# Storing tile 13 of a 16-tile head in two halves

## The chip, the cores and the metric

The kernel runs on one core of a Trainium2 chip. The metric is the device time of one execution in microseconds (us), the median of several runs.

## The reference

```
users, items = interactions[:, 0], interactions[:, 1]          # 2048 pairs
all_embed = concatenate([users_emb_w[users], items_emb_w[items]], axis=1)   # 32 + 32
h = relu(all_embed @ w1.T + b1)                                 # 128
h = relu(h @ w2.T + b2)                                         # 128
cross = one_hot(items, 1250)
return sigmoid(concatenate([cross, h], axis=1) @ w_head.T + b_head)   # 2048 x 1250 f32
```

The product with the one-hot part is a choice of one row of the head's weights. So each pair needs a gathered row of 1250 numbers, the product of h with the remaining 128 columns of the head, the bias, and a sigmoid. 10.24 MB of output are written.

## The kernel before, in words

The 2048 pairs are 16 tiles of 128 (t = 0 to 15, LAST = 15). For each tile GpSimd issues two indirect DMAs (L167, L171): one brings the item's embedding and its 1250 head numbers, the other the user's embedding, into the tile's part of `rows`. Every tile has its own 1250 columns there, `logits(t)`; the sum, the sigmoid and the store all work in that place. A gather is issued when the one four tiles before it has landed.

VectorE splits the embedding into two parts of fewer bits (L206, L208), TensorE transposes it (L301), VectorE copies it back (L212). TensorE then does layer 1 (L309, L310), ScalarE relu 1 (L262), TensorE layer 2 (L314), ScalarE relu 2 twice, once rounded (L266) and once in full (L271), and VectorE takes their difference (L216). The head is four passes over 1250 columns, in chunks of 512, 512 and 226, into one of two PSUM accumulators (L318). VectorE adds the gathered row (`add_rows`, L221), ScalarE applies the sigmoid (`sigmoid`, L275), and SyncE, which waits for the sigmoid, issues the store (L144).

The order on each engine is written out by hand. For t = 1 to 14, ScalarE does relu 1 and relu 2 of tile t+1 and then the sigmoid of tile t-1, so that the sigmoid of tile 13 stands behind both layers' relus of tile 15. VectorE does the sum of tile t-1, the preparation of tile t+2 and then the difference for tile t+1.

The end is written differently. Tile 14 is added, put through the sigmoid and stored in two halves of 625 columns (L240, L288, L148). Tile 15 goes in three chunks, for which TensorE computes one chunk after the other (`last_head`, L350), VectorE adds (L244), ScalarE applies the sigmoid (L292), and the chunks are stored by SyncE (L152) and, the last, by ScalarE's own queue (L295). SyncE issues stores strictly in order, each behind its wait; its last wait is for all stores to have landed (L153).

Of the kernel before, what the change touches and what calls it, by code (L numbers as in the profile page):

```python
# [7 lines left out]
SLOTS = 2  # L8
IN_FLIGHT = 4
WARM = 6  # L10

ALU = mybir.AluOpType
ACT = mybir.ActivationFunctionType
# [5 lines left out]
def rec_head_kernel(nc, pairs, user_rows, item_rows, w1T, b1, w2T, b2, w_hiddenT, b_head, out):  # L19
# [5 lines left out]
    H2, N = w_hiddenT.shape  # L25
# [3 lines left out]
    TILES = B // P  # L29
    LAST = TILES - 1  # L30
# [2 lines left out]
    chunks = [(c, min(BANK, N - c)) for c in range(0, N, BANK)]  # L33
    halves = [(0, N // 2), (N // 2, N - N // 2)]
    BANKS = len(chunks)
    assert B % P == 0 and H1 == P and H2 == P and 2 * K1 == P and item_rows.shape[1] == ITEM_ROW
    assert BP * BC == N and TILES > IN_FLIGHT

# [4 lines left out]
    with ExitStack() as ctx:  # L43
# [6 lines left out]
        def sem(name):  # L50
            return ctx.enter_context(nc.semaphore(name))
# [60 lines left out]
        s_acc = sem("s_acc")  # L112
        s_sum = sem("s_sum")
        s_prob = sem("s_prob")
        s_out = sem("s_out")
        s_half_sum = sem("s_half_sum")
        s_half_prob = sem("s_half_prob")
        s_last_acc = sem("s_last_acc")
        s_last_sum = sem("s_last_sum")
        s_last_prob = sem("s_last_prob")  # L120

        def embedding(t):
            return rows[:, t * ROW:t * ROW + K1]
# [1 line left out]
        def logits(t, c=0, n=N):  # L125
            return rows[:, t * ROW + K1 + c:t * ROW + K1 + c + n]
# [3 lines left out]
        @block.sync  # L130
        def _(sp):
            sp.dma_start(idx[:], pairs_v).then_inc(s_idx, 16)
            sp.dma_start(bias_f[:], bias_v).then_inc(s_bhead, 16)
            for half in range(2):
                sp.dma_start(w1T_f[half * K1:(half + 1) * K1, :], w1T).then_inc(s_w1, 16)
            sp.dma_start(w2T_sb[:], w2T).then_inc(s_w2, 16)
            sp.wait_ge(s_const, 3)
            sp.wait_ge(s_bias_split, 2)
            for r, part in enumerate((bias_hi, bias_lo)):
                sp.dma_start(bias_parts[r:r + 1, :].bitcast(F32).rearrange("a (p c) -> a p c", p=BP),  # L140
                             part[:].bitcast(F32)).then_inc(s_bias_row, 16)
            for t in range(LAST - 1):
                sp.wait_ge(s_prob, t + 1)
                sp.dma_start(out_v[:, t * N:(t + 1) * N], logits(t)).then_inc(s_out, 16)  # L144

            for i, (c, n) in enumerate(halves):
                sp.wait_ge(s_half_prob, i + 1)
                sp.dma_start(out_v[:, (LAST - 1) * N + c:(LAST - 1) * N + c + n],  # L148
                             logits(LAST - 1, c, n)).then_inc(s_out, 16)
            for i, (c, n) in enumerate(chunks[:-1]):  # L150
                sp.wait_ge(s_last_prob, i + 1)
                sp.dma_start(out_v[:, LAST * N + c:LAST * N + c + n], logits(LAST, c, n)).then_inc(s_out, 16)  # L152
            sp.wait_ge(s_out, 16 * (LAST - 1 + len(halves) + BANKS))  # L153

        @block.gpsimd
        def _(pool):
# [19 lines left out]
        @block.vector  # L176
        def _(dve):
            nc.vector.memset(warm_pe[:], 0.0).then_inc(s_warm_pe, 1)  # L178
            nc.vector.memset(warm[:], 0.0).then_inc(s_const, 1)
            nc.vector.memset(bias_sel[:].bitcast(F32), 0.0).then_inc(s_const, 1)  # L180
            nc.vector.memset(bias_parts[:].bitcast(F32), 0.0).then_inc(s_const, 1)
            dve.wait_ge(s_const, 3)
            nc.vector.memset(bias_sel[0:2, :].bitcast(F32), 1.0).then_inc(s_const, 1)
            dve.wait_ge(s_bhead, 16)
            nc.vector.tensor_copy(bias_hi[:], bias_f[:]).then_inc(s_bias_split, 1)
            dve.wait_ge(s_bias_split, 1)
            nc.vector.tensor_tensor(bias_lo[:], bias_f[:], bias_hi[:].bitcast(F32),
                                    ALU.subtract).then_inc(s_bias_split, 1)
            dve.wait_ge(s_w1, 32)
            nc.vector.tensor_copy(w1T_hi[:], w1T_f[:]).then_inc(s_w1_parts, 1)  # L190
            dve.wait_ge(s_w1_parts, 1)
            nc.vector.tensor_tensor(w1T_lo[:], w1T_f[:], w1T_hi[:].bitcast(F32), ALU.subtract).then_inc(s_w1_parts, 1)

            def split_hidden():

                dve.wait_ge(s_hid_hi, 1)
                dve.wait_ge(s_hid_f, 1)
                nc.vector.tensor_tensor(w_hid_lo[:], acc[1][:, 0:N], w_hid_hi[:].bitcast(F32),
                                        ALU.subtract).then_inc(s_hid_lo, 1)

            def split_emb(t):
                dve.wait_ge(s_rows[t], 32)
                if t >= 1:

                    dve.wait_ge(s_xT, t)
                nc.vector.tensor_copy(emb[:, 0:K1].bitcast(F32R), embedding(t)).then_inc(s_emb_hi, 1)  # L206
                dve.wait_ge(s_emb_hi, t + 1)
                nc.vector.tensor_tensor(emb[:, K1:2 * K1], embedding(t), emb[:, 0:K1], ALU.subtract).then_inc(s_emb, 1)  # L208

            def copy_embT(t):  # L210
                dve.wait_ge(s_xT, t + 1)
                nc.vector.tensor_copy(embT[:], ps_x[:, 0:P]).then_inc(s_embT, 1)  # L212

            def split_h2(t):
                dve.wait_ge(s_h2, t + 1)
                nc.vector.tensor_tensor(h2T_lo[t % SLOTS][:], h2T_f[:], h2T_hi[t % SLOTS][:].bitcast(F32),  # L216
                                        ALU.subtract).then_inc(s_h2_lo, 1)

            def add_rows(t):
                dve.wait_ge(s_acc, t + 1)  # L220
                nc.vector.tensor_tensor(logits(t), acc[t % SLOTS][:, 0:N], logits(t), ALU.add).then_inc(s_sum, 1)  # L221

            split_emb(0)
            copy_embT(0)
            split_hidden()
            split_emb(1)
            copy_embT(1)
            split_h2(0)
            split_emb(2)
            copy_embT(2)  # L230
            split_h2(1)
            for t in range(1, LAST):
                add_rows(t - 1)
                if t + 2 < TILES:
                    split_emb(t + 2)
                    copy_embT(t + 2)
                split_h2(t + 1)
            dve.wait_ge(s_acc, LAST)
            for c, n in halves:
                nc.vector.tensor_tensor(logits(LAST - 1, c, n), acc[(LAST - 1) % SLOTS][:, c:c + n],  # L240
                                        logits(LAST - 1, c, n), ALU.add).then_inc(s_half_sum, 1)
            for i, (c, n) in enumerate(chunks):
                dve.wait_ge(s_last_acc, i + 1)
                nc.vector.tensor_tensor(logits(LAST, c, n), acc[LAST % SLOTS][:, c:c + n], logits(LAST, c, n),  # L244
                                        ALU.add).then_inc(s_last_sum, 1)

        @block.scalar
        def _(act):
# [11 lines left out]
            def relu_1(t):  # L260
                act.wait_ge(s_l1, t + 1)
                nc.scalar.activation(h1T[:], ps_h[:, 0:P], ACT.Relu, bias=b1_sb[:]).then_inc(s_h1, 1)  # L262
# [7 lines left out]
                    act.wait_ge(s_h2_lo, t)  # L270
                nc.scalar.activation(h2T_f[:], ps_h[:, P:2 * P], ACT.Relu, bias=b2_sb[:]).then_inc(s_h2, 1)  # L271

            def sigmoid(t):
                act.wait_ge(s_sum, t + 1)
                nc.scalar.activation(logits(t), logits(t), ACT.Sigmoid).then_inc(s_prob, 1)  # L275

            act.wait_ge(s_b12, 32)
            relu_1(0)
# [2 lines left out]
            relu_2(1)  # L281
            for t in range(1, LAST):
                relu_1(t + 1)
                relu_2(t + 1)
                sigmoid(t - 1)
            for i, (c, n) in enumerate(halves):
                act.wait_ge(s_half_sum, i + 1)
                nc.scalar.activation(logits(LAST - 1, c, n), logits(LAST - 1, c, n),  # L288
                                     ACT.Sigmoid).then_inc(s_half_prob, 1)
            for i, (c, n) in enumerate(chunks):  # L290
                act.wait_ge(s_last_sum, i + 1)
                nc.scalar.activation(logits(LAST, c, n), logits(LAST, c, n), ACT.Sigmoid).then_inc(s_last_prob, 1)  # L292
            c, n = chunks[-1]
            act.wait_ge(s_last_prob, BANKS)
            act.dma_start(out_v[:, LAST * N + c:LAST * N + c + n], logits(LAST, c, n)).then_inc(s_out, 16)  # L295

        @block.tensor
        def _(pe):
# [22 lines left out]
            def bias_pass(t):  # L321
                if t == 1:

                    pe.wait_ge(s_hid_lo, 1)
                if t >= SLOTS:
                    pe.wait_ge(s_sum, t - SLOTS + 1)
                one_pass(t, bias_sel[:], bias_parts, True, False)

            def hi_pass(t):
# [10 lines left out]
            def last_head(t):  # L340
                s = t % SLOTS
                hi = h2T_hi[s][:]
                lo = h2T_lo[s][:]
                pe.wait_ge(s_sum, t - SLOTS + 1)
                pe.wait_ge(s_h2_hi, t + 1)
                pe.wait_ge(s_h2_lo, t + 1)
                terms = [(bias_sel[:], bias_parts), (hi, w_hid_hi), (hi, w_hid_lo), (lo, w_hid_hi)]
# [69 lines left out]
```

## Time and profile before

| | |
|---|---|
| runs shown | 68.83, 69.0, 69.25 us; median 69.0 |
| profiled execution, its own time | 68.38 us |
| span in the trace (first to last instruction) | 66.5 us |
| granted TensorE clock over the span | 0.998 |
| busy: TensorE, VectorE, ScalarE, GpSimd | 57.2, 42.1, 38.5, 31.3 us |
| HBM read and written | 11.56 MB and 10.24 MB |

The span is shorter than the execution's own time by 1.9 us, which lie around it. The times in the rows are counted from the span's start and come from this one execution. A row of a timeline has the start, the duration, engine, line and operation, destination and sources, shape and count, and in brackets how long the engine had been idle and what released it. SPq and ACTq are the queues on which SyncE and ScalarE issue DMAs.

### The profile page before, as it was taken

The numbers are of one execution on the slowest core, as the hardware profiler recorded it, in microseconds if no ns is written. First come the engines' busy times: TensorE is split into PE (matmuls) and PEld (weight loads), VectorE is DVE, ScalarE is ACT, GpSimd is POOL, SyncE is SP. The second block draws the span as 40 slices with busy tenths as digits, with TensorE's granted clock in tenths as the row PEclk, the third lists the DMA queues.
The fourth block names the chain that finished last, engine by engine and source line by source line (L and its number), as shares of the span: only waits on it lengthen the run. The fifth ranks groups of instructions, "written<-read, shape, count | busy, mean of one in ns | idle before, by whom it ended". The sixth has DMA issues, their size and how long they took to land.

```text
span 66.5 us, 864 instructions
## 1 busy us (share of the span) xinstructions
PE 57.2 (86%) x284; PEld 42.7 (64%) x284; DVE 42.1 (63%) x93; ACT 38.5 (58%) x71; POOL 31.3 (47%) x38
## 2 busy tenths in 40 slices
PE   1999976999999997959999999999999998998000
PEld 1344355776888885838886888787877867876000
DVE  3811167558869684936795969586868676579200
ACT  0713904336667659372586666849494857589600
POOL 4287787687687688688686755550000000000000
PEclk9999999999999999999999999999999999999999
DMA  0489998898999899899999999999999996717992
GB/s 0 53 322 342 279 334 271 192 346 265 210 371 357 294 395 402 261 406 419 417 421 409 421 422 417 414 421 417 425 416 407 410 417 243 319 72 313 383 374 85
DMA packets 6496, 21.86 MB, mean 329 GB/s; under 512 B 1372, under 2 KB 2012, under 8 KB 6492
## 3 DMA queue, kind: packets, MB, share of 16 engines
q0 software_dynamic: 2816, 10.77, 46.4%
q1 hardware_dynamic: 3100, 10.29, 38.8%
q10 hardware_dynamic: 576, 0.76, 3.8%
q8 instruction: 2, 0.03, 0.2%
q14 instruction: 2, 0.02, 0.1%
HBM read 11.56 MB, written 10.24 MB: 328 GB/s over the span
## 4 chain that ended last, share of the span: by engine, by line
DMA 33%; POOL 33%; issue 13%; PE 6%; ACT 4%; DVE 2%; POOLq 2%
DMA rows<-user_rows,idx 30%; POOL rows L167 17%; POOL rows L171 16%; PE acc L318 4%; DMA idx<-pairs 3%; ACT rows L288 2%; ACT rows L292 2%; POOLq L43 2%; DVE rows L240 1%; PE ps_h L314 0%; PE ps_x L301 0%; DVE emb L208 0%; DVE emb L206 0%; PE ps_h L310 0%; PE ps_h L309 0%
## 5 line engine op out<-in xcount | busy, mean ns | idle before, releaser
L221 DVE TENSOR_TENSOR rows<-acc,rows 128x1250 f32<-128x1250 f32 x14 | 20.4, 1459 | 1.1
L167 POOL DMA_INDIRECT rows<-item_rows,idx x16 | 15.4, 964 | 7.4 <-issue 3.7
L275 ACT ACTIVATE rows<-rows 128x1250 f32<-128x1250 f32 x14 | 17.5, 1248 | 0.0
L171 POOL DMA_INDIRECT rows<-user_rows,idx x16 | 15.1, 947 | 4.9 <-issue 4.9
L318 PE MATMUL acc<-w_hid_lo,h2T_hi 128*128 128x512 f32 (+1 forms) x45 | 12.3, 381 | 0.0
L318 PE MATMUL acc<-w_hid_hi,h2T_lo 128*128 128x512 f32 (+1 forms) x45 | 12.2, 379 | 0.0
L318 PE MATMUL acc<-w_hid_hi,h2T_hi 128*128 128x512 f32 (+1 forms) x45 | 11.8, 369 | 0.0
L262 ACT ACTIVATE h1T<-ps_h,b_sb 128x128 f32<-128x128 f32 x16 | 5.9, 367 | 9.9 <-PE ps_h L310 9.9
L318 PE MATMUL acc<-bias_parts,bias_sel 128*128 128x512 f32 (+1 forms) x45 | 11.3, 359 | 0.0
L266 ACT ACTIVATE h2T_hi<-ps_h,b_sb 128x128 fp32r<-128x128 f32 x16 | 5.9, 368 | 9.3 <-PE ps_h L314 9.3
L212 DVE CAST embT<-ps_x 128x128 fp32r<-128x128 f32 x16 | 4.7, 293 | 7.5 <-PE ps_x L301 7.5
L356 PE MATMUL ps_x<-warm_pe 128*128 128x512 f32 x12 | 7.1, 751 | 1.5 <-DVE warm_pe L178 1.5
L318 PEld LDWEIGHTS acc<-w_hid_hi,h2T_lo 128*128 128x128 f32 x45 | 7.9, 201 | 0.7
L314 PE MATMUL ps_h<-h1T,w2T_sb 128*128 128x128 f32 x32 | 7.8, 325 | 0.6 <-ACT h1T L262 0.6
L318 PEld LDWEIGHTS acc<-bias_parts,bias_sel 128*128 128x128 f32 x45 | 7.3, 189 | 1.3
L318 PEld LDWEIGHTS acc<-w_hid_lo,h2T_hi 128*128 128x128 f32 x45 | 7.4, 191 | 0.7
L318 PEld LDWEIGHTS acc<-w_hid_hi,h2T_hi 128*128 128x128 f32 x45 | 7.4, 190 | 0.6
L314 PEld LDWEIGHTS ps_h<-h1T,w2T_sb 128*128 128x128 f32 x32 | 4.8, 188 | 2.9 <-issue 0.7
L301 PE MATMUL ps_x<-ident,emb 128*128 128x128 f32 x16 | 4.9, 306 | 1.9 <-DVE emb L208 1.8
L206 DVE CAST emb<-rows 128x64 fp32r<-128x64 f32 x16 | 3.2, 199 | 5.2 <-DMA rows<-user_rows,idx 5.1
L356 PEld LDWEIGHTS ps_x<-warm_pe 128*128 128x128 f32 x12 | 2.8, 247 | 4.9 <-issue 3.4
L301 PEld LDWEIGHTS ps_x<-ident,emb 128*128 128x128 f32 x16 | 2.2, 139 | 5.6 <-DVE emb L208 4.1
(39 smaller groups left out, 50.3 us busy)
## 6 DMA issues: line engine op xcount, KB each, us to landing
probs<-rows SPq DMA_DIRECT2D x14, 625.0 KB, 7.2
w_hid_f<-w_hiddenT ACTq DMA_DIRECT2D x1, 625.0 KB
probs<-rows SPq DMA_DIRECT2D x2, 312.5 KB, 3.0
probs<-rows SPq DMA_DIRECT2D x2, 256.0 KB, 3.4
rows<-item_rows,idx POOLq DMA_INDIRECT x16, 7.4
rows<-user_rows,idx POOLq DMA_INDIRECT x16, 7.8
probs<-rows ACTq DMA_DIRECT2D x1, 113.0 KB, 3.5
w1T_f<-w1T SPq DMA_DIRECT2D x2, 32.0 KB
```

Of the source, the lines that this page charges most:

```text
L167: nc.gpsimd.indirect_dma_start(out=rows[:, at + UD:at + ROW], out_offset=None, in_=item_rows, in_offset=bass.IndirectOffsetOnAxis(ap=idx[: ...
L171: nc.gpsimd.indirect_dma_start(out=rows[:, at:at + UD], out_offset=None, in_=user_rows, in_offset=bass.IndirectOffsetOnAxis(ap=idx[:, 2 * ...
L206: nc.vector.tensor_copy(emb[:, 0:K1].bitcast(F32R), embedding(t)).then_inc(s_emb_hi, 1)
L212: nc.vector.tensor_copy(embT[:], ps_x[:, 0:P]).then_inc(s_embT, 1)
L221: nc.vector.tensor_tensor(logits(t), acc[t % SLOTS][:, 0:N], logits(t), ALU.add).then_inc(s_sum, 1)
L262: nc.scalar.activation(h1T[:], ps_h[:, 0:P], ACT.Relu, bias=b1_sb[:]).then_inc(s_h1, 1)
L266: nc.scalar.activation(h2T_hi[t % SLOTS][:], ps_h[:, P:2 * P], ACT.Relu, bias=b2_sb[:]).then_inc(s_h2_hi, 1)
L275: nc.scalar.activation(logits(t), logits(t), ACT.Sigmoid).then_inc(s_prob, 1)
L301: nc.tensor.transpose(ps_x[:, 0:P], emb[:], ident[:]).then_inc(s_xT, 1)
L314: nc.tensor.matmul(ps_h[:, P:2 * P], w2T_sb[:], h1T[:], start=True, stop=True).then_inc(s_l2, 1)
L318: last = nc.tensor.matmul(acc[t % SLOTS][:, c:c + n], h, w[:, c:c + n], start=first, stop=end)
L356: nc.tensor.matmul(ps_x[:], warm_pe[:, 0:P], warm_pe[:], start=True, stop=True)
```

## The change

`HALVED` names tiles 13 and 14. A list `parts` gives the pieces of every tile: one of 1250 columns for tiles 0 to 12, two of 625 for tiles 13 and 14, the three chunks for tile 15. The sum, the sigmoid and the store of a tile walk over its pieces, and one pair of semaphores, `s_sum` and `s_prob`, counts pieces for all tiles, where there were three pairs. On ScalarE the first half of tile 13's sigmoid stands between relu 1 and relu 2 of tile 15, the second half behind relu 2. Tiles 14 and 15 had their pieces before.

```
+HALVED = (13, 14)
+    parts = [halves if t in HALVED else [(0, N)] for t in range(LAST)] + [chunks]
+    def parts_until(t):
+        return sum(len(p) for p in parts[:t + 1])
 (SyncE)
-            for t in range(LAST - 1):
-                sp.wait_ge(s_prob, t + 1)
-                sp.dma_start(out_v[:, t * N:(t + 1) * N], logits(t)).then_inc(s_out, 16)
 ...
+            for t in range(TILES):
+                for i, (c, n) in enumerate(parts[t][:-1] if t == LAST else parts[t]):
+                    sp.wait_ge(s_prob, parts_until(t - 1) + i + 1)
+                    sp.dma_start(out_v[:, t * N + c:t * N + c + n], logits(t, c, n)).then_inc(s_out, 16)
+            sp.wait_ge(s_out, 16 * parts_until(LAST))
 (VectorE)
             def add_rows(t):
-                dve.wait_ge(s_acc, t + 1)
-                nc.vector.tensor_tensor(logits(t), acc[t % SLOTS][:, 0:N], logits(t), ALU.add).then_inc(s_sum, 1)
+                if t < LAST:
+                    dve.wait_ge(s_acc, t + 1)
+                for i, (c, n) in enumerate(parts[t]):
+                    if t == LAST:
+                        dve.wait_ge(s_last_acc, i + 1)
+                    nc.vector.tensor_tensor(logits(t, c, n), acc[t % SLOTS][:, c:c + n], logits(t, c, n),
+                                            ALU.add).then_inc(s_sum, 1)
 (ScalarE)
+            def sigmoid(t, i):
+                c, n = parts[t][i]
+                act.wait_ge(s_sum, parts_until(t - 1) + i + 1)
+                nc.scalar.activation(logits(t, c, n), logits(t, c, n), ACT.Sigmoid).then_inc(s_prob, 1)
 ...
             for t in range(1, LAST):
                 relu_1(t + 1)
+                if t - 1 in HALVED:
+                    sigmoid(t - 1, 0)
                 relu_2(t + 1)
-                sigmoid(t - 1)
+                sigmoid(t - 1, len(parts[t - 1]) - 1)
 (TensorE, bias_pass and last_head)
-                pe.wait_ge(s_sum, t - SLOTS + 1)
+                pe.wait_ge(s_sum, parts_until(t - SLOTS))
```

## Rows read from the trace of the kernel before

**Rows 1.** Chain that ended last, in order of time: start, us, what

```profile
43.32 11.22 DMA rows<-user_rows,idx
...
54.56 0.21 DVE emb L206
...
57.68 1.17 PE acc L318 x6
58.84 0.02 issue
58.87 0.82 DVE rows L240
59.69 0.02 issue
59.71 1.44 ACT rows L288 x2
61.15 1.43 ACT rows L292 x3
```

**Rows 2.** Windows: stretch, us, engines' busy (instructions), clock, DMA share, GB/s

```profile
34.00:54.00 20.00, 19.89 (x111) 15.78 (x110) 15.44 (x31) 13.55 (x26) 6.78 (x8) 1.00 1.02 416
56.95:58.55 1.60, 1.60 (x10) 1.29 (x9) 0.70 (x2) 1.02 (x4) 0.00 (x0) 1.00 1.00 400
58.60:60.25 1.65, 1.65 (x8) 1.24 (x7) 1.45 (x3) 1.42 (x2) 0.00 (x0) 1.00 0.00 0
60.25:60.32 0.07, 0.07 (x2) 0.04 (x1) 0.07 (x2) 0.07 (x1) 0.00 (x0) 1.00 0.00 0
60.25:61.85 1.60, 1.09 (x7) 0.79 (x5) 1.60 (x4) 1.60 (x4) 0.00 (x0) 1.00 0.98 400
61.85:63.52 1.67, 0.00 (x0) 0.00 (x0) 0.08 (x1) 0.73 (x2) 0.00 (x0) 1.00 1.00 379
63.52:65.25 1.73, 0.00 (x0) 0.00 (x0) 0.00 (x0) 0.00 (x0) 0.00 (x0) 1.00 1.00 371
```

**Rows 3.** Stores as issued, SyncE's and ScalarE's queues, timeline

```profile
56.15 0.33 SPq L144 DMA_DIRECT2D probs<-rows  x1
...
59.50 0.33 SPq L144 DMA_DIRECT2D probs<-rows  x1
60.47 0.33 SPq L148 DMA_DIRECT2D probs<-rows  x1
62.61 0.35 ACTq L295 DMA_DIRECT2D probs<-rows  x1
```

**Rows 4.** Stores issued at 59.50, 60.47, 62.61: size, us from issue to landing

```profile
probs<-rows SPq DMA_DIRECT2D x1, 625.0 KB, 2.9
probs<-rows SPq DMA_DIRECT2D x1, 312.5 KB, 2.9
probs<-rows ACTq DMA_DIRECT2D x1, 113.0 KB, 3.5
```

**Rows 5.** Timeline of ScalarE from 56.7 us

```profile
56.77 0.37 ACT L262 ACTIVATE h1T<-ps_h,b_sb 128x128 f32<-128x128 f32 x1 [0.65 <-PE ps_h L310]
57.71 0.37 ACT L266 ACTIVATE h2T_hi<-ps_h,b_sb 128x128 fp32r<-128x128 f32 x1 [0.58 <-PE ps_h L314]
57.98 0.36 ACT L271 ACTIVATE h2T_f<-ps_h,b_sb 128x128 f32<-128x128 f32 x1
58.23 1.25 ACT L275 ACTIVATE rows<-rows 128x1250 f32<-128x1250 f32 x1
59.71 0.73 ACT L288 ACTIVATE rows<-rows 128x625 f32<-128x625 f32 x1 [0.23 <-DVE rows L240]
60.42 0.73 ACT L288 ACTIVATE rows<-rows 128x625 f32<-128x625 f32 x1
61.06 0.61 ACT L292 ACTIVATE rows<-rows 128x512 f32<-128x512 f32 x1
```

**Rows 6.** Timeline of VectorE, the same stretch

```profile
56.01 1.46 DVE L221 TENSOR_TENSOR rows<-acc,rows 128x1250 f32<-128x1250 f32 x1
58.37 0.29 DVE L216 TENSOR_TENSOR h2T_lo<-h2T_f,h2T_hi 128x128 fp32r<-128x128 f32 x1 [0.90 <-ACT h2T_f L271]
58.87 0.81 DVE L240 TENSOR_TENSOR rows<-acc,rows 128x625 f32<-128x625 f32 x1 [0.20 <-PE acc L318]
59.59 0.80 DVE L240 TENSOR_TENSOR rows<-acc,rows 128x625 f32<-128x625 f32 x1
```

**Rows 7.** Timeline of TensorE: tile 14's last pass, tile 15's first and last matmul

```profile
58.09 0.74 PE L318 MATMUL acc<-w_hid_hi,h2T_lo 128*128 128x512 f32 x3
58.81 0.47 PE L350 MATMUL acc<-bias_parts,bias_sel 128*128 128x512 f32 x1
61.07 0.27 PE L350 MATMUL acc<-w_hid_hi,h2T_lo 128*128 128x226 f32 x1
```

More of the change, by code:

```diff
@@ L115, in rec_head_kernel @@
         s_out = sem("s_out")
-        s_half_sum = sem("s_half_sum")
-        s_half_prob = sem("s_half_prob")
         s_last_acc = sem("s_last_acc")
-        s_last_sum = sem("s_last_sum")
-        s_last_prob = sem("s_last_prob")
         def embedding(t):
@@ L141, in _ @@
                              part[:].bitcast(F32)).then_inc(s_bias_row, 16)
-            for t in range(LAST - 1):
-                sp.wait_ge(s_prob, t + 1)
-                sp.dma_start(out_v[:, t * N:(t + 1) * N], logits(t)).then_inc(s_out, 16)
[L146 to L153, printed above, removed]
+            for t in range(TILES):
[3 more added lines that the diff above has]
+            sp.wait_ge(s_out, 16 * parts_until(LAST))
         @block.gpsimd
@@ L237, in _ @@
                 split_h2(t + 1)
[L238 to L245, printed above, removed]
+            add_rows(LAST - 1)
+            add_rows(LAST)
         @block.scalar
@@ L271, in relu_2 @@
                 nc.scalar.activation(h2T_f[:], ps_h[:, P:2 * P], ACT.Relu, bias=b2_sb[:]).then_inc(s_h2, 1)
-            def sigmoid(t):
-                act.wait_ge(s_sum, t + 1)
-                nc.scalar.activation(logits(t), logits(t), ACT.Sigmoid).then_inc(s_prob, 1)
+            def sigmoid(t, i):
+                c, n = parts[t][i]
+                act.wait_ge(s_sum, parts_until(t - 1) + i + 1)
+                nc.scalar.activation(logits(t, c, n), logits(t, c, n), ACT.Sigmoid).then_inc(s_prob, 1)
             act.wait_ge(s_b12, 32)
@@ L283, in _ @@
                 relu_1(t + 1)
+                if t - 1 in HALVED:
+                    sigmoid(t - 1, 0)
                 relu_2(t + 1)
-                sigmoid(t - 1)
[L286 to L294, printed above, removed]
+                sigmoid(t - 1, len(parts[t - 1]) - 1)
+            for t in range(LAST - 1, TILES):
+                for i in range(len(parts[t])):
+                    sigmoid(t, i)
+            c, n = parts[LAST][-1]
+            act.wait_ge(s_prob, parts_until(LAST))
             act.dma_start(out_v[:, LAST * N + c:LAST * N + c + n], logits(LAST, c, n)).then_inc(s_out, 16)
@@ L343, in last_head @@
                 lo = h2T_lo[s][:]
-                pe.wait_ge(s_sum, t - SLOTS + 1)
+                pe.wait_ge(s_sum, parts_until(t - SLOTS))
                 pe.wait_ge(s_h2_hi, t + 1)
```

## The prediction

> **What bounds the kernel now.** I read the chain of waits first, then the windows of the last 10 us, then the queues' timelines there. The chain [rows 1] runs through the gathers to the landing of tile 15's rows at 54.54 us, goes through tile 15's preparation and tile 14's last passes (57.68), the sum and sigmoid of tile 14's halves, and ends with tile 15's sigmoids at 62.58. From this view alone the end looks like compute. But the span goes on to 66.5, and the chain does not say why those last 3.9 us are so long.
>
> The windows [rows 2] say it. From 34 to 54 us the 16 DMA engines are full (share 1.02, 416 GB/s): gathers and stores share them. Tile 12's store fills 56.95 to 58.55. Then the engines stand still until after 60.32, and from there they are full again to 65.25: 1.60 us at 400 GB/s, which is tile 13's 640 KB, 1.67 us at 379, which is tile 14's 640 KB, and 1.73 us at 371, which is tile 15's 640 KB. The last sigmoid is over 2.7 us before the last of these bytes moves. A second sign: the last store, 113 KB, took 3.5 us to land, while tile 13's 625 KB, issued into idle engines, took 2.9 [rows 4]. It stood in a backlog. So the end is set by the time at which the backlog begins and by its volume, 1.92 MB in 4.95 us, not by ScalarE or VectorE.
>
> The backlog begins with tile 13's store. It is issued at 59.50 [rows 3], 0.02 us after its sigmoid (58.23 + 1.25 = 59.48) [rows 5], and its first packet moves after 60.32, so 0.83 us from issue to first packet. The sigmoid is that late because it is one piece behind relu 2 of tile 15, while ScalarE was idle for 0.58 us just before that relu, and tile 13's sum had begun at 56.01 [rows 5, 6].
>
> **The change part by part.** The sum: tile 13's add of 1.46 us becomes two of 0.81 and 0.80 that begin 0.72 apart, as tile 14's do (59.59 - 58.87) [rows 6]. The first is done at 56.01 + 0.81 = 56.82, the second at 56.01 + 0.72 + 0.80 = 57.53, 0.06 later than the whole sum was. What is behind it on VectorE is the difference for tile 15 at 58.37, which waits for relu 2; TensorE needs the sum before it overwrites the accumulator at 58.81 [rows 7]. The 0.06 is hidden by both, over 0.8 us off.
>
> The sigmoid's first half: ScalarE can begin it behind relu 1 of tile 15. Relu 1 starts at 56.77, and an instruction behind a relu starts 0.25 to 0.27 later (57.71, 57.98, 58.23) [rows 5], so at 57.03; the sum was there at 56.82. It takes 0.73 [rows 5] and ends at 57.76.
>
> What is queued behind it is relu 2 of tile 15, the one place where this edit can hurt. TensorE lets relu 2 go at 57.71. No row shows a relu behind a 625-wide sigmoid. Nearest: an instruction starts 0.64 after a sigmoid of 625 (60.42 to 61.06), and VectorE may have set that start. That gives 57.67, no delay at all. If there is no overlap, relu 2 starts at 57.78 (57.03 + 0.73, and 0.02 for the wait), 0.07 late. For an upper bound I take a whole sigmoid, 0.73 late, though nothing in the trace looks like it. I take 0, the nearest row. A delay is free up to 0.19: behind relu 2 is the difference for tile 15 (58.37 + 0.29 = 58.66 at its end), and the next add waits for TensorE's pass over tile 14 and starts at 58.87 anyway [rows 6, 7], so it would have to be more than 0.2 late. TensorE's tile 15 would start later by the delay, and that is hidden in the backlog: tile 15's last chunk was issued at 62.61 and could move at 63.44, long before its turn.
>
> The sigmoid's second half starts where the whole one did, 58.23, and ends at 58.96. ScalarE is free 0.52 earlier, which brings nothing to tile 14: its sigmoid waited 0.23 for VectorE's add at 59.71 [rows 5].
>
> The stores: SyncE had one issue and has two, each of 0.33 us. They are issued at 57.78 and 58.98; the next one, tile 14's, at 60.47 as before [rows 3]. SyncE has time for all of them. With 0.83 from issue to first packet the first half could move from 58.61, just as tile 12's store is through (58.55). For packets of 2500 bytes I take tile 14's rate, 379 GB/s: 320 KB in 0.84 us. So the first half is moved from 58.61 to 59.45, the second from 59.81 to 60.65. Both lie in the stretch that is empty now and end before tile 14 can start.
>
> That is the new limit. Tile 14's first half is issued at 60.47, and its first packet can't move before 60.47 + 0.83 = 61.30. In the kernel before it moved at 61.85, when tile 13 was through. From here on everything is as before: 1.28 MB in 1.67 + 1.73 = 3.40 us, so the last bytes move at 64.70 instead of 65.25. Tile 14's second half, issued 0.71 behind the first, has 0.84 us of cover from it, tile 15's chunks more. The sum is -0.55 us. Tile 13's store took 1.60 us out of the end; 0.55 of it is gained, and what is left turns into idle engines from 60.65 to 61.30, in which nothing is there to be stored.
>
> Bounds of this term hang on the time from issue to first packet. There is a second reading, tile 12's store: issued at 56.15 [rows 3], moving from 56.95 [rows 2], 0.80. From the rows it is at least the issue's own 0.33, which would let tile 14 move from 60.80, a gain of 1.05; and at most what the landing leaves beside the movement, 2.9 - 1.6 = 1.3 [rows 2, 4], which gives 61.77 and a gain of 0.08. Two readings agree to 0.03, so I stay at 0.83.
>
> The profiled execution would go from 68.38 to 67.83. It is 0.62 below the median of the runs. The term is a difference between two stages of the same tail, so I carry it over whole: 69.0 - 0.55 = 68.45.
>
> The Trainium skill, "DMA: Bandwidth & Descriptors", "Rules for kernel authors", asks for at least 1 MiB per DMA for bandwidth and for many small transfers to be coalesced. It speaks against cutting a store of 625 KB in two. Its section on the anatomy of one DMA fits about 2.0 us plus bytes by 436 GB/s to one transfer (of the GpSimd path); if a second half paid these 2.0 us on the path, the time would be 69.0 - 0.55 + 2.0 = 70.45. The rows bear out only a small part of that: see the last rival.
>
> **The rivals.** (a) No gain. The end follows ScalarE after all, as the chain says, or the halves of tile 13 don't reach the engines in the empty stretch. For: the chain ends in L292. Against: the DMA share of 1.00 for 2.7 us behind it. Time 69.0.
>
> (b) The half sigmoid delays relu 2 of tile 15 by all of its 0.73. Then the difference is done at 59.39, tile 14's add starts at 59.41 instead of 58.87, and tile 14's first store is issued 0.54 later: 61.01 + 0.83 = 61.84, against 61.85 before. The gain is gone: 69.0. Half of such a delay leaves 68.6. Against: the sum is ready 0.21 us before ScalarE gets there, and the gap before relu 2 is 0.58 wide.
>
> (c) Slower: the gather stage shifts. The stores and the gathers share full engines until 54.54, and tile 15's gather took 11.22 us to land [rows 1]. If the new order of instructions lets one more store of 1.60 us go ahead of that gather, everything behind it moves: 69.0 + 1.60 - 0.55 = 70.05. It decides from a landing that is 0.55 late. Against: up to there the waits and the issues of all queues are the same, one for one. The same shift the other way would give 66.85.
>
> (d) Slower: a store has a fixed price that the DMA engines pay one after the other. Tile 13's store landed in 2.9 us, of which 1.60 were movement, so 1.3 at most; one more store gives 69.0 - 0.55 + 1.3 = 69.75. Against: tile 14's and tile 15's five stores moved back to back at a share of 1.00, with no 1.3 between them. This is what the skill's rule on coalescing would make of the change.
>
> **How the numbers follow.** Forecast 0.73, (a) 0.10, (b) 0.09, (c) 0.05 and 0.01 for its opposite, (d) 0.02. What a measurement can tell from no change is 0.5%, 0.35 us, so faster is below 68.65. The forecast with its bounds (a gain of 0.08 to 1.05, most of it near 0.55) lies there with 0.63 of its 0.73, the rest is "same". All of (a) and 0.08 of (b) are "same". Faster: 0.63 + 0.01 + 0.01 = 0.65; same: 0.10 + 0.10 + 0.08 = 0.28; slower: 0.05 + 0.02 = 0.07. The range goes from 68.0 (a gain of 1.0, about the bound) to 69.1, which takes in (a) and (b) and leaves out (c) and (d).
>
> **What would show it.** In the trace after: tile 13's first sigmoid at 57.0 and relu 2 of tile 15 still at 57.7; tile 13's stores issued near 57.8 and 59.0; the DMA engines moving 320 KB each near 58.6 to 59.45 and 59.8 to 60.65, a short gap, then full from 61.3 to 64.7; the last store, still issued at 62.6, landing in about 2.95 instead of 3.5 us. The forecast is wrong if relu 2 is over 0.2 late, if tile 14's first half starts to move later than 61.6, or if tile 15's rows land at another time than 54.5.

## The result and the profile after

In the first comparison the changed kernel took 68.13 us (67.97 to 68.33, 4 runs) and the kernel before 69.09 (68.83 to 69.25, 4 runs): ratio 0.9871, interval 0.9827 to 0.9914. It is faster by 0.96 us, where 0.55 was forecast (68.45). Three more comparisons further down gave 0.997, 0.9931 and 0.9991; the intervals of two of the four leave out 1. Medians are over all runs, while a ratio is that of the fast runs (within about 1.5% of the kernel's fastest), so the two need not agree. The profiled execution took 67.97 us, with a span of 66.2 us.

ScalarE around tile 15's relus, in the timeline of the changed kernel (columns as ahead of the prediction; it answers to [rows 5]):

```profile
57.13 0.37 ACT L259 ACTIVATE h1T<-ps_h,b_sb 128x128 f32<-128x128 f32 x1 [0.62 <-PE ps_h L307]
57.40 0.72 ACT L273 ACTIVATE rows<-rows 128x625 f32<-128x625 f32 x1
58.08 0.37 ACT L263 ACTIVATE h2T_hi<-ps_h,b_sb 128x128 fp32r<-128x128 f32 x1
58.34 0.36 ACT L268 ACTIVATE h2T_f<-ps_h,b_sb 128x128 f32<-128x128 f32 x1
58.59 0.72 ACT L273 ACTIVATE rows<-rows 128x625 f32<-128x625 f32 x1
60.07 0.73 ACT L273 ACTIVATE rows<-rows 128x625 f32<-128x625 f32 x1 [0.75 <-DVE rows L223]
```

The half sigmoid fills the gap between relu 1 and relu 2. Relu 2 starts 0.95 us behind relu 1 (58.08 - 57.13), and it did so before (57.71 - 56.77 = 0.94): not delayed. The wait in front of tile 14's sigmoid grew from 0.23 to 0.75, and its start did not move: 2.94 behind relu 1 in both.

All of this stands 0.36 us later in the span than before, because tile 15's rows landed at 54.91 us in this execution and not at 54.54 (chain, start and us; it answers to the first line of [rows 1]):

```profile
44.14 10.77 DMA rows<-user_rows,idx
```

So times in different traces are counted from the start of relu 1 of tile 15, which is 56.77 in the kernel before and 57.13 here.

The stores of the changed kernel as issued (timeline), and for two of them the size and the time to landing: the first line holds for the store issued at 58.14 and for that at 60.83, the second for the last one (against [rows 3] and [rows 4]):

```profile
58.14 0.33 SPq L150 DMA_DIRECT2D probs<-rows  x1
59.34 0.33 SPq L150 DMA_DIRECT2D probs<-rows  x1
60.83 0.33 SPq L150 DMA_DIRECT2D probs<-rows  x1
62.98 0.35 ACTq L292 DMA_DIRECT2D probs<-rows  x1
```

```profile
probs<-rows SPq DMA_DIRECT2D x1, 312.5 KB, 2.2
...
probs<-rows ACTq DMA_DIRECT2D x1, 113.0 KB, 2.8
```

Windows of the changed kernel (columns as in [rows 2]; a packet counts where it starts):

```profile
57.36:58.96 1.60, 1.60 (x11) 1.24 (x9) 0.76 (x2) 1.60 (x5) 0.00 (x0) 1.00 1.01 400
58.99:59.95 0.96, 0.96 (x5) 0.67 (x4) 0.77 (x2) 0.33 (x1) 0.00 (x0) 1.00 0.87 331
59.95:60.18 0.23, 0.23 (x2) 0.19 (x1) 0.23 (x2) 0.11 (x1) 0.00 (x0) 1.00 0.00 0
60.18:61.10 0.92, 0.92 (x5) 0.75 (x4) 0.92 (x2) 0.92 (x2) 0.00 (x0) 1.00 0.89 348
61.12:61.65 0.53, 0.53 (x5) 0.41 (x3) 0.53 (x2) 0.53 (x2) 0.00 (x0) 1.00 0.00 0
61.65:65.18 3.53, 0.07 (x1) 0.00 (x0) 0.66 (x2) 1.29 (x3) 0.00 (x0) 0.87 0.96 363
65.18:66.10 0.92, 0.00 (x0) 0.00 (x0) 0.00 (x0) 0.00 (x0) 0.00 (x0) 0.50 0.00 0
```

Read from the top: tile 12's store, tile 13's first half right behind it, a gap, tile 13's second half, a gap of 0.53 us, and then 3.53 us for tiles 14 and 15. The long empty stretch in front of the backlog [rows 2] is gone; what is left of it stands in two small gaps. (A window's start or end is up to 0.02 us beside the packet that it is meant for.) Tile 14's first half was issued at 60.83, its first packet moved at 61.66: 0.83 us, as read in the kernel before. After the last packet 0.98 us pass until the span ends at 66.16.

### The profile page after: what moved, and what is told of

It is laid out like the page before. It is cut to its first block, busy times and chain, and to the rows that moved or that the text cites. A ratio compares the mean times of both kernels' runs of the same rounds, so it can differ in the third digit from the quotient of the medians.

```text
span 66.2 us, 867 instructions
## 1 busy us (share of the span) xinstructions
PE 57.4 (87%) x284; PEld 43.0 (65%) x284; DVE 42.0 (63%) x94; ACT 38.6 (58%) x72; POOL 31.2 (47%) x38
## 4 chain that ended last, share of the span: by engine, by line
DMA 34%; POOL 33%; issue 13%; PE 6%; ACT 4%; DVE 2%; POOLq 2%
DMA rows<-user_rows,idx 31%; POOL rows L165 17%; POOL rows L169 16%; PE acc L315 4%; ACT rows L273 4%; DMA idx<-pairs 3%; POOLq L51 2%; DVE rows L223 1%; PE ps_h L311 0%; PE ps_x L298 0%; DVE emb L206 0%; DVE emb L204 0%; PE ps_h L307 0%; PE ps_h L306 0%
## 5 line engine op out<-in xcount | busy, mean ns | idle before, releaser
L223 DVE TENSOR_TENSOR rows<-acc,rows 128x1250 f32<-128x1250 f32 (+3 forms) x20 | 23.6, 1197 | 1.2 <-PE acc L315 0.2
L273 ACT ACTIVATE rows<-rows 128x1250 f32<-128x1250 f32 (+3 forms) x20 | 20.5, 1037 | 0.8 <-DVE rows L223 0.8
L353 PE MATMUL ps_x<-warm_pe 128*128 128x512 f32 x12 | 7.8, 817 | 1.5 <-DVE warm_pe L176 1.5
L268 ACT ACTIVATE h2T_f<-ps_h,b_sb 128x128 f32<-128x128 f32 x16 | 5.8, 360 | 0.0
```

The lines of the kernel that those rows point to most:

```text
L223: nc.vector.tensor_tensor(logits(t, c, n), acc[t % SLOTS][:, c:c + n], logits(t, c, n), ALU.add).then_inc(s_sum, 1)
L273: nc.scalar.activation(logits(t, c, n), logits(t, c, n), ACT.Sigmoid).then_inc(s_prob, 1)
L353: nc.tensor.matmul(ps_x[:], warm_pe[:, 0:P], warm_pe[:], start=True, stop=True)
```

## The experiments

The first four kernels ran on one chip at 69 us for the kernel before. The other eight ran at another level: all took 97 to 98 us, the kernel before too. In the one trace read for it, what differs lies in the first 50 us (see the last section). The tail of the changed kernel is the same at both levels to some hundredths, and so is that of (c), so tails are compared across the levels. No trace of the kernel before was taken at the 98 us level: its tail is known from 69 us, from its own trace and from (a). Times are medians; each interval is that of the ratio to the kernel before.

**Only the counting rewritten (a).** Tile 13 in one piece.

```
-HALVED = (13, 14)
+HALVED = (14,)
```

> Only the rewritten counting of pieces, tile 13 in one piece as before. Theory 1 (all of the gain is tile 13's earlier bytes, the rest of the 0.96 is the spread of the gather stage): same as the kernel before, 0.0 us (between -0.3 and +0.3), first packet of tile 14 again behind tile 13's last one. Rival (part of the gain comes from the rewritten counting or from the instructions being laid out differently): 0.3 to 0.4 us faster than before, seen in the stretch up to the landing of tile 15's rows or outside the span.

69.04 us against 69.02, ratio 1.0014 (0.9973 to 1.0056). Its windows show the long gap and the backlog again:

```profile
59.30:60.64 1.34, 1.34 (x7) 1.08 (x7) 1.34 (x3) 1.11 (x2) 0.00 (x0) 1.00 0.00 0
60.65:65.72 5.07, 1.02 (x7) 0.74 (x5) 1.61 (x4) 2.25 (x5) 0.00 (x0) 0.97 0.98 379
```

The last packets move at 8.61 behind relu 1, against 8.62 in the kernel before. So the rewritten counting brings nothing to the time that this interval could show, and nothing to the last packets. What the change gives there, the halving gives.

**The changed kernel again, three times (b).**

> The changed kernel again. Theory 1: 0.55 us faster than before (0.35 to 0.75), and from the landing of tile 15's rows to the end of the span about 0.55 to 0.6 less than before. Rival: 0.96 again, with the other 0.4 at one and the same place.

68.80 us against 69.02, ratio 0.997 (0.993 to 1.001). That is a gain of about 0.2, below the 0.35 to 0.75 expected; from the landing of tile 15's rows (55.09) to the end it is 11.34 us against 12.00, 0.66 less, where 0.55 to 0.6 was expected.

> The changed kernel a third time. Theory 1 (the tail gains 0.57 us, and the time of tile 15's landing varies from run to run in both kernels alike): 0.57 faster than before, with 0.3 to either side; last bytes again 10.25 us after tile 15's first cast, and not at 10.82 as before. Rival (the change also moves the gather stage): the landing of tile 15's rows in this trace is away from 54.5 to 55.1 us.

97.42 us against 97.94, ratio 0.9931 (0.9896 to 0.9967). The rival's sign can't be read here, since at this level relu 1 of tile 15 stands at 86.40 for a reason that is open (last section). Counted from tile 15's first cast the last packets move at 10.36 and not at 10.25: at this level that cast comes 0.13 us earlier before relu 1, and the tail behind relu 1 is the same.

> The changed kernel beside three of its relatives. Theory 1: 0.57 us less tail than before; the time 0.57 less within the spread of the landings (0.3 either way), last bytes 10.25 after tile 15's first cast. Rival (the first comparison's 0.96 is the size): 0.96 again.

97.61 us against 97.93, ratio 0.9991 (0.9948 to 1.0034). The last stretch of the three, windows of each kernel in turn:

```profile
61.83:65.36 3.53, 0.06 (x1) 0.00 (x0) 0.64 (x2) 1.29 (x3) 0.00 (x0) 0.88 0.96 363
```

```profile
90.92:94.44 3.52, 0.05 (x1) 0.00 (x0) 0.64 (x2) 1.28 (x3) 0.00 (x0) 0.95 0.96 364
```

```profile
90.53:94.07 3.54, 0.05 (x1) 0.00 (x0) 0.64 (x2) 1.29 (x3) 0.00 (x0) 0.90 0.96 362
```

The fourth comparison fell below its expectation too (0.09 for 0.57 with 0.3 to either side).

With relu 1 of tile 15 at 57.31, 86.40 and 86.02 the last packets move at 8.04, 8.03 and 8.05 behind it, and at 8.04 in the first trace. In the kernel before it is 8.62 (a few packets follow the last window of [rows 2], the last of them ends at 65.39), in (a) 8.61. The last packets gain 0.57 us every time. The four ratios (0.89, 0.21, 0.68 and 0.09 us below the kernel before, 0.47 on average) don't repeat like that. In the second comparison the runs of the changed kernel spread over 0.8 us and those of the kernel before over 2.6, while the time outside the span is 1.8 us in all. The rival's 0.96 didn't come again.

**Both half sigmoids behind relu 2 (c).**

```
-                if t - 1 in HALVED:
-                    sigmoid(t - 1, 0)
                 relu_2(t + 1)
-                sigmoid(t - 1, len(parts[t - 1]) - 1)
+                for i in range(len(parts[t - 1])):
+                    sigmoid(t - 1, i)
```

> Tile 13 in two halves, but both sigmoids behind relu 2 of tile 15. Theory 1: the halves are issued 1.2 and 0.6 later than in the changed kernel, move without a gap from 59.8 to 61.5 (times of the kernel before), and tile 14 starts 0.2 later than in the changed kernel: 0.36 us faster than before, 0.2 slower than the changed kernel. Rival (the place between the relus is what counts): no gain over before.

69.18 us against 69.02, ratio 1.0003 (0.9953 to 1.0053): the interval ends at a gain of 0.32, short of the 0.36 expected. In its trace tile 15's rows landed at 56.02. Repeated:

> Tile 13 in halves, both sigmoids behind relu 2 of tile 15. Its tail was 0.41 shorter than that of before, while its time was the same. Theory 1 (the time differed by late landings only): 0.41 faster than before within 0.3. Rival (what the tail gains is lost elsewhere): the same as before again, with landings of tile 15's rows late again (56.0).

97.55 us against 97.93, ratio 0.9945 (0.9896 to 0.9993). Windows of the repeated kernel, with its relu 1 at 86.42:

```profile
88.80:89.44 0.64, 0.64 (x4) 0.54 (x3) 0.64 (x2) 0.50 (x2) 0.00 (x0) 1.00 0.00 0
89.45:94.62 5.17, 1.56 (x9) 1.16 (x7) 2.15 (x4) 2.78 (x5) 0.00 (x0) 0.97 0.98 371
```

Tile 13 starts earlier than before and the backlog is without a gap. The last packets move at 8.20 and 8.19, 0.42 earlier than before and 0.15 later than in the changed kernel; 0.36 and 0.2 were expected. From the last packet to the end of the span 1.26 us pass in both of its traces, against 1.15 before and 0.90 to 1.08 in the changed kernel. So the end comes at 9.47 in both, and 0.2 to 0.3 is left of the gain (9.77 before, 9.64 in (a)). The halving alone starts the bytes earlier; the place between the relus gives the rest, 0.15 on the last packets and 0.44 on the end. The two traced executions took 69.52 and 97.69 us, each above its median.

**Tile 13 not stored at all (h).** This kernel leaves out tile 13's two stores, and the last wait counts two landings fewer; everything else is the changed kernel.

```
                 for i, (c, n) in enumerate(...):
+                    if t == 13:
+                        continue
                     sp.wait_ge(s_prob, parts_until(t - 1) + i + 1)
 ...
-            sp.wait_ge(s_out, 16 * parts_until(LAST))
+            sp.wait_ge(s_out, 16 * (parts_until(LAST) - 2))
```

> The changed kernel without tile 13's two stores: its 128 rows are not written. Theory 1 (in the changed kernel the end hangs on the issue of tile 14's first half and no longer on the volume of tile 13): the same as the changed kernel within 0.1 us, though 640 KB less are written. Rival (the end still hangs on the volume in the DMA queues): up to 1.05 us faster than the changed kernel.

68.17 us against 69.02, ratio 0.9896 (0.9844 to 0.9948). Its windows, with relu 1 at 57.93:

```profile
59.95:62.46 2.51, 2.51 (x13) 2.02 (x12) 2.43 (x4) 1.76 (x4) 0.00 (x0) 1.00 0.00 0
62.46:65.97 3.51, 0.06 (x1) 0.00 (x0) 0.65 (x2) 1.29 (x3) 0.00 (x0) 0.84 0.97 365
```

Its last packets move at 8.04, to the hundredth where the changed kernel has them, though 640 KB less were stored and the engines stood still for 2.51 us. This is the clearest proof of the forecast's middle step: with the change tile 13's bytes no longer hold up the last packets, which hang on the issue of tile 14's first half. The end of the span is at 8.91 against 8.94 to 9.12.

The time of whole runs doesn't say the same: 68.17 is 0.63 below the 68.80 of the changed kernel in the same comparison, where no more than 0.1 either way was expected. At most 0.2 of that stands in the tails of the two traces. The rest would have to lie in front of relu 1 of tile 15, where both kernels issue the same; the one trace here has that relu later (57.93 against 57.31), so it doesn't show where, and the 0.4 us stay open.

**The whole sigmoid between the relus (d).**

```
-HALVED = (13, 14)
+HALVED = (14,)
 ...
-                if t - 1 in HALVED:
+                if t - 1 == 13:
                     sigmoid(t - 1, 0)
                 relu_2(t + 1)
-                sigmoid(t - 1, len(parts[t - 1]) - 1)
+                if t - 1 != 13:
+                    sigmoid(t - 1, 0)
```

> Tile 13 in one piece, its whole sigmoid between relu 1 and relu 2 of tile 15. Theory 1 (tile 14's first store sets the end, and a delay of relu 2 reaches it through the difference for tile 15 on VectorE): relu 2 about 0.9 us late, tile 14's first store issued about 0.75 later, counted from the landing of tile 15's rows; last bytes 0.75 later than in the changed kernel and 0.2 later than before. Rival (a late relu 2 is hidden, the volume alone counts): as fast as the changed kernel.

97.92 us against 97.94, ratio 1.0017 (0.9972 to 1.0062). ScalarE's and VectorE's timelines and the last windows:

```profile
86.04 0.37 ACT L259 ACTIVATE h1T<-ps_h,b_sb 128x128 f32<-128x128 f32 x1 [0.23 <-PE ps_h L307]
86.78 1.25 ACT L273 ACTIVATE rows<-rows 128x1250 f32<-128x1250 f32 x1 [0.37 <-DVE rows L223]
87.94 0.35 ACT L263 ACTIVATE h2T_hi<-ps_h,b_sb 128x128 fp32r<-128x128 f32 x1
```

```profile
88.57 0.29 DVE L214 TENSOR_TENSOR h2T_lo<-h2T_f,h2T_hi 128x128 fp32r<-128x128 f32 x1 [1.83 <-ACT h2T_f L268]
88.78 0.80 DVE L223 TENSOR_TENSOR rows<-acc,rows 128x625 f32<-128x625 f32 x1
```

```profile
90.58:91.19 0.61, 0.61 (x6) 0.53 (x5) 0.37 (x2) 0.61 (x2) 0.00 (x0) 1.00 0.00 0
91.19:94.73 3.54, 0.36 (x4) 0.18 (x2) 0.95 (x2) 1.30 (x3) 0.00 (x0) 1.00 0.97 362
```

The sigmoid waits 0.37 for the whole sum, and relu 2 starts 1.90 behind relu 1 instead of 0.95. Tile 14's first add starts 2.74 behind relu 1 (88.78), where it was 2.10 before (58.87 [rows 6]), and its first store is issued 0.63 later than in the changed kernel. Tile 14 starts to move 5.15 behind relu 1 instead of 4.52 (starts of the windows), and the last packets move at 8.68, 0.64 later than in the changed kernel and 0.06 later than before. The late relu 2 does reach the end, by the path that the prediction's rival (b) describes; 0.75 was expected for it. The difference is that the add started 0.21 behind the start of the tile's difference, whose row is 0.29 long, and did not wait for that row's end: a delay of relu 2 is free up to 0.95 - 0.64 = 0.3 us and not 0.19. This is also why the halving is needed at all: with a whole sigmoid in that place the last packets are as late as before. (The end of the span is at 9.59, against 9.64 and 9.77 with tile 13 whole in its old place and 9.03 in the changed kernel.)

**Tile 14 in pieces of 512, 512 and 226 (f).**

```
+    parts[14] = chunks
```

> The changed kernel with tile 14 in pieces of 512, 512 and 226 columns instead of two of 625. Theory 1: the first store of tile 14 is issued 0.24 earlier (a sum of 0.69 for 0.81, a sigmoid of 0.61 for 0.73) and the last bytes move 0.24 earlier than in the changed kernel. Rival (the end no longer hangs on this issue): no difference.

97.49 us against 97.94, ratio 0.9902 (0.9861 to 0.9943). Repeated:

> Tile 14 in pieces of 512, 512 and 226. Theory 1: last bytes 0.13 to 0.24 earlier than in the changed kernel, counted from tile 15's first cast. Rival: the additional store makes the landing of the last one later by as much, so that the span from that cast is the same.

97.60 us against 97.93, ratio 0.9951 (0.9896 to 1.0007). Windows of the repeated kernel, with relu 1 at 87.22:

```profile
91.22:91.51 0.29, 0.29 (x4) 0.29 (x3) 0.29 (x2) 0.29 (x2) 0.00 (x0) 1.00 0.00 0
91.51:95.13 3.62, 0.29 (x3) 0.11 (x1) 0.88 (x2) 1.53 (x4) 0.00 (x0) 1.00 0.95 354
```

The backlog starts at 4.29 instead of 4.52, about the 0.24 that were expected, and takes 0.1 longer; the last packets move at 7.90 and 7.91, 0.13 earlier than in the changed kernel, about half of the first expectation. But the end of the span is at 9.05 and 9.08, no earlier than 9.03, the mean of the four traces of the changed kernel. Here the rival was right: the time after the last packet grew to 1.14 and 1.17.

**Tile 14 in pieces of 313, 469 and 468 (g).**

```
+    parts[14] = [(0, 313), (313, 469), (782, 468)]
```

> The changed kernel with tile 14 in pieces of 313, 469 and 468 columns. Theory 1: the first store of tile 14 is issued about 0.65 earlier and goes on right behind tile 13's second half; the limit passes to tile 14's second piece and tile 15's first chunk, and the last bytes move 0.45 earlier than in the changed kernel, about 1.0 earlier than before. Rival: no difference from the changed kernel.

97.03 us against 97.94, ratio 0.989 (0.9853 to 0.9927). Repeated:

> Tile 14 in pieces of 313, 469 and 468. Theory 1: last bytes 0.27 earlier than in the changed kernel, the limit being tile 15's first chunk, whose store is issued at 7.2 to 7.3 after tile 15's first cast; 0.85 faster than before. Rival: as fast as the changed kernel, since the time from the last byte to the last landing is longer by as much.

96.99 us against 97.93, ratio 0.9902 (0.9845 to 0.9958). A window of the repeated kernel from tile 13's second half on, with relu 1 at 86.05:

```profile
88.28:91.90 3.62, 2.36 (x12) 1.80 (x11) 2.95 (x6) 3.13 (x6) 0.00 (x0) 1.00 0.91 343
```

There is no long gap any more: share 0.91 over 3.62 us. The last packets move at 7.76 and 7.75, 0.28 earlier than in the changed kernel, where 0.45 were expected for the first run. The end comes at 9.04 and 8.92, a mean of 8.98 against 9.03. In both comparisons the interval against the kernel before leaves out 1, at a gain of 1%. Its medians are also 0.4 and 0.6 below those of the changed kernel beside it, but the tail explains 0.05 of that; whether it is better than the changed kernel stays open.

## Why the prediction was right, and what of it was not

**The bound.** Right, as far as the last packets go. The backlog of stores set the end, not the sigmoids in which the chain of waits ends. In the changed kernel ScalarE's last sigmoid stands where it stood, 5.8 us behind relu 1, and the end comes 0.5 to 0.8 earlier. The prediction's windows stop a little short of the last packets (65.25 for 65.39), so its 3.40 us for tiles 14 and 15 is 3.5 in both kernels. That drops out of the difference.

**ScalarE.** The half sigmoid was expected at 0.26 behind relu 1 and came at 0.27; relu 2 was not delayed (0.95 behind relu 1), in any of four traces. Experiment (d) shows what lies past that cover, which is 0.3 and not 0.19 wide.

**The stores.** Issued at 1.01, 2.21 and 3.70 behind relu 1 (58.14, 59.34, 60.83), against forecasts of 1.01, 2.21 and 3.70. From issue to first packet 0.83 in tile 14. The two halves of tile 13 took 0.96 and 0.92 us each instead of 0.84; a half with no store behind it ran at 331 and 348 GB/s in its window and not at the 379 of the backlog. It cost nothing, as the gaps took it.

**The sum.** The forecast let the backlog of tiles 14 and 15 move 0.55 earlier. Measured 0.57 (8.62 to 8.04 or 8.05), four times, with the kernel before traced at the 69 us level only.

**The signs.** The prediction named three signs against it. Read as times of the span, all three came: relu 2 stood at 58.08 for 57.71, tile 14's first half started to move at 61.66, past 61.6, and tile 15's rows landed at 54.91 and not at 54.5. All are the same shift of 0.36 us. Without it relu 2 is on time and tile 14 moves at 61.30, as forecast. The signs were tied to times of the span, and these vary from execution to execution.

**The size.** Two terms were missing. The forecast held the time from the last packet to the end of the span constant. It was 1.15 and 1.03 with tile 13 whole (before, a) and 0.98, 1.08, 0.90 and 0.97 with the change, on average 0.1 less. So the tail from relu 1 to the end went from 9.77 and 9.64 to 9.03 on average, 0.68 us. The other term is the base: the prediction carried its 0.55 over to the median of three runs, 0.6 above the profiled execution of before. That execution (68.38) was shorter than each of the 33 timed runs of the kernel before in the two comparisons at this level (68.4 at the lowest), so its rows probably landed early for this kernel. The changed kernel's profiled execution was 67.97, near the forecast of 67.83 for it; between the two spans stand 0.36 later at relu 1 and 0.74 less behind it. The 0.3 us between 0.68 and the 0.96 measured is not in the tail. Since (a) moved nothing, and since the next three comparisons gave 0.21, 0.68 and 0.09 us, it is most likely the spread of the stage in front of tile 15's landing, in four runs of each kernel. That is argued; the single traces kept here can't show it. That 68.13 lies inside the forecast's range, 0.13 above its lower bound, is in part luck.

**The rivals.** (a), no gain, is refuted for the tail by the four traces; of the four ratios alone, two could be no gain. (b) is a real mechanism (0.64 measured for a delay of 0.95, where the whole sigmoid stands in the way), but the half sigmoid does not set it off. Its price was put too high: by the cover of 0.3 a delay of 0.73 would cost about 0.4, by this estimate, and not 0.54. (c), the gather stage: relu 1 of tile 15 came 0.36 and 0.54 us later than in the one trace of before, with the counting alone 0.32, in (h) 1.16 and in the first (c) 1.47. It was not one store more: in all six traces at 69 us SyncE had issued eight stores ahead of tile 15's second gather and twelve by its landing. Since it also comes with tile 13 whole (a), and since the one traced execution of before was shorter than all its timed runs, it is most likely the spread of the runs; more traces of before would be needed to show it. (d), a price per store on the path: one more store and no 1.3 us; in (g) two more than before and the last packets 0.87 earlier. A much smaller price may sit behind the last packet (see the last section). The Trainium skill, "DMA: Bandwidth & Descriptors", "Rules for kernel authors", says to coalesce many small transfers into a large one. Read as the prediction read it, the time should have risen; the traces disagree for stores that move beside others, and agree in small with the 331 and 348 GB/s of tile 13's halves.

## What to carry to other kernels

When the chain of waits ends in compute, look at the transfers behind it: here a small last store that took longer to land than a large earlier one stood in a backlog, and the start of the backlog was what to move. Cutting the piece behind the idle stretch helps only until the next store's issue becomes the limit; here leaving that store out altogether gave the same last packets. And count a change of half a microsecond inside the trace, from an event that the change doesn't touch: the last packets of one kernel repeated to 0.02 us where the ratios of whole runs scattered over a percent.

## What the runs showed of the hardware that was not expected

The time from the last packet to the end of the span is not constant: 0.87 (h), 0.90 (d), 0.90 to 1.08 (changed), 1.03 (a) and 1.15 (before), 1.14 and 1.17 (f), 1.16 and 1.27 (g), 1.26 twice (c). It ate most of what (f) and (g) won. The order goes by the number of stores that move without a long gap up to the end: five in (h), (d) and the changed kernel, six in (a), before and (f), seven in (c), eight or more in (g). The means are 0.95, 1.12, 1.26 and 1.22, so 0.14 to 0.17 us for a store more, up to seven. It is read from these traces only; no experiment varied the number alone, and the cause is open.

At the 98 us level the chain of waits of the changed kernel (third run) has three long stretches early on that no engine of this core explains:

```profile
13.86 9.74 another core or an unknown queue
...
24.11 5.12 another core or an unknown queue
...
31.07 17.10 another core or an unknown queue
```

```profile
31.00:48.00 17.00, 4.16 (x12) 3.19 (x12) 0.07 (x1) 1.61 (x4) 9.04 (x10) 0.60 0.73 222
52.00:80.00 28.00, 28.00 (x159) 23.71 (x158) 21.22 (x48) 19.59 (x37) 0.00 (x0) 0.98 0.51 207
```

From 31 to 48 us (its windows) TensorE worked 4.16 of 17 us at a granted clock of 0.60, and from 52 to 80 it was busy all the time with the DMA engines half idle, so that there TensorE and not the gathers led up to the tail. The same last packets came out, at 8.03 behind relu 1. Where the stretches come from stays open; the kernel before was at the same level in those comparisons.
